# Graph network layer on one core: stages of the main loop set one group of gathers apart, early messages' bias on TensorE and relu on ScalarE

## What is computed

```python
src = node_feature[edge_src]
parts = [jax.nn.relu(node_feature)]
for t in range(n_types):
    msg = jax.nn.relu(src @ W_e[t].T + b_e[t])
    msg = jnp.where((edge_type == t)[:, None], msg, jnp.zeros((), msg.dtype))
    parts.append(jax.ops.segment_sum(msg, edge_dst, num_segments=N))
agg = jnp.concatenate(parts, axis=1)
for t in range(n_types):
    o = agg @ W_n[t].T + b_n[t]
    updated = jnp.where((node_type == t)[:, None], o, updated)
# then: x = layernorm(x + updated + node_feature)
```

## Time and profile before

| What | us |
|---|---|
| median of 3 runs | 922.02 (919.35 to 922.12) |
| span of the profiled execution | 1076.0 |
| PE, DVE, POOL, ACT busy in it | 771.1, 683.5, 671.4, 149.6 |
| mean granted TensorE clock in it | 0.872 |

### The profile page before, as it was taken

How to read it: one execution, slowest core, us unless ns; L and a number is a source line. 1 busy time by engine, 2 the same in 40 slices (tenths; PEclk the granted TensorE clock), 3 DMA queues, 4 the chain that set the end, 5 groups by cost and what they waited for, 6 DMA issues and landing times. The chain is left out here.

```text
span 1076.0 us, 13097 instructions
## 1 busy us (share of the span) xinstructions
PE 771.1 (72%) x4200; PEld 611.8 (57%) x4200; DVE 683.5 (64%) x1539; ACT 149.6 (14%) x397; POOL 671.4 (62%) x718
## 2 busy tenths in 40 slices
PE   5574267777778778777676686888787786778866
PEld 3242156666666566566555565666566565566654
DVE  7997866666555656656566565656656654465645
ACT  2264101101101101100110110011011001111101
POOL 7776655666566666665666665666666666665660
PEclk9697578978898998998999988989888978898898
DMA  7476312422222223223223223223223233132320
GB/s 219 135 256 190 81 50 60 86 72 67 78 80 75 71 77 85 72 70 89 71 70 93 74 67 91 71 67 96 72 67 108 71 105 90 45 93 70 87 57 16
DMA packets 65777, 94.03 MB, mean 87 GB/s; under 512 B 16497, under 2 KB 49233, under 8 KB 65711
## 3 DMA queue, kind: packets, MB, share of 16 engines
q0 software_dynamic: 22432, 45.99, 17.2%
q1 hardware_dynamic: 40577, 43.14, 13.0%
q10 hardware_dynamic: 2702, 4.08, 1.3%
HBM read 80.23 MB, written 12.92 MB: 87 GB/s over the span
## 5 line engine op out<-in xcount | busy, mean ns | idle before, releaser
L619 POOL DMA_INDIRECT tab<-message_table,idx_t x630 | 594.3, 943 | 353.0 <-issue 170.4
L1116 DVE TENSOR_TENSOR work<-key_t,ps 128x378 f32<-128x378 f32 (+1 forms) x180 | 109.5, 610 | 253.1 <-remote 133.0
L1516 PE MATMUL ps<-work,tab 128*128 128x126 f32 x1260 | 197.4, 304 | 35.4 <-DVE acc L1125 20.6
L1516 PEld LDWEIGHTS ps<-work,tab 128*128 128x128 f32 x1260 | 183.3, 219 | 50.3 <-DVE acc L1125 25.5
L1546 PE MATMUL ps<-we_t,order_f 128*128 128x128 f32 x540 | 115.4, 368 | 123.2 <-DVE order_f L1204 84.1
L1546 PEld LDWEIGHTS ps<-we_t,order_f 128*128 128x128 f32 x540 | 93.3, 255 | 135.6 <-DVE order_f L1204 88.8
L1595 PE MATMUL ps<-wn_t,stage 128*128 128x384 f32 x294 | 104.6, 493 | 0.0
L1204 DVE TENSOR_TENSOR order_f<-ps,dst_raw 128x768 f32<-128x768 f32 x45 | 43.1, 957 | 71.7 <-remote 56.7
L615 POOL DMA_INDIRECT xg<-in_x,esrc_t x67 | 71.0, 1060 | 23.9 <-issue 17.7
L1595 PEld LDWEIGHTS ps<-wn_t,stage 128*128 128x128 f32 x294 | 56.3, 193 | 39.7 <-issue 3.1
L747 ACT ACTIVATE dense_f<-ps 128x256 f32<-128x256 f32 x45 | 17.2, 383 | 432.7 <-PE ps L1548 228.8
(11 more groups left out here) (231 smaller groups left out, 952.2 us busy)
## 6 DMA issues: line engine op xcount, KB each, us to landing
tab<-message_table,idx_t POOLq DMA_INDIRECT x630
message_table<-tab SPq DMA_DIRECT2D x24, 384.0 KB
dst_raw<-dense_types SPq DMA_DIRECT2D x45, 192.0 KB
wn_raw<-message_table SPq DMA_DIRECT2D x22, 384.0 KB
src_wide<-dense_lists SPq DMA_DIRECT2D x45, 128.0 KB
xg<-in_x SPq DMA_DIRECT2D x11, 256.0 KB
work<-in_x ACTq DMA_DIRECT2D x10, 256.0 KB
out<-xg SPq DMA_DIRECT2D x10, 256.0 KB
```

Of the source, the lines that this page charges most:

```text
L619: pool.indirect_dma_start(msg[:, slot, :], None, table, bass.IndirectOffsetOnAxis(ap=rows, axis=0)).then_inc(signal, 16)
L1116: dve.tensor_tensor(hot[:, first:first + n, :].rearrange("p c (t w) -> p c t w", w=WIN), keys.broadcast_to((P, n, T, WIN)), iota_win.rearr ...
L1516: ins = pe.matmul(sums_bank(nth), msg[:, column, :], hot[:, column, :], start=(c == 0), stop=(c == n - 1))
```

## The change

Every engine's `iteration` is rewritten, with functions of their own for iterations 0, 1 and the last. In the steady iteration TensorE now does, after g0: `early_make`, `dense_make`; after g1: `dense_turn` of the next iteration; after g2: half of the dense sum, the linear part, `finish_turn`; after g3: the other half, `early_sum`, `early_turn`, `place_selfs`. Between two steps of one item that stand on TensorE there is now at least one group's sum. Groups keep fixed banks (g0 and g2 bank 0, g1 and g3 bank 1); early and dense sums get columns of their own in those banks, and all adds are counted by one semaphore `added`, by a list (`adds_of`). The early messages' bias becomes a bf16 matmul (line 1539 of after), the relu one ScalarE instruction over both chunks, `early_select` and the type masks made for it in setup are gone, and `early_sum` has a matmul for each type and chunk, 42 columns wide. SP loads the next dense lists ahead of the self rows, and the first load of x takes two tiles (`BATCHES`).

```diff
-            link(dve.tensor_copy(etype_i[:, :, :], ekey_t[:, :, :]))
-            link(dve.tensor_scalar(etype_i[:, :, :], etype_i[:, :, :], BITS, None, ALU.logical_shift_right))
             for t in range(T):
-                dve.tensor_scalar(emask[:, :, :, t], etype_i[:, :, :], float(t), None, ALU.is_equal)
...
+            def iteration_one():
...
+                for side in range(SETS):
+                    dense_add(0, side, first_of[2 * side], added_by(1, "p" + str(side)))
+                self_types()
+
+                dve.wait_ge(group_summed, NG + 3)
+                one_hot(2, 2)
+                add_group(1, 2, bases_of[2])
+                dense_mask(1)
+                dense_hot(1)
+
+                dve.wait_ge(group_summed, NG + 4)
+                one_hot(2, 3)
+                dve.wait_ge(e_summed, 1)
+                add_group(1, 3, bases_of[3])
+                early_add(0, bases_of[NG])
+                early_hot(1)
+                self_masks()
+                for side in range(SETS):
+                    dense_add(1, side, bases_of[2 * side], added_by(1, "d" + str(side)))
...
+            def iteration(j, extra=None, last_extra=None):
+                early = j <= NE
+                bases_of = load_bases(j, early)
+
+                dve.wait_ge(group_summed, NG * j + 1)
+                one_hot(j + 1, 0)
+                add_group(j, 0, bases_of[0])
+                dense_onehot(j + 1)
+                finish_acc(j - 2, j - 2, 0, ADDS_BEFORE[j])
                 if j > 2:
...
+                    finish_y(j - 3, j - 3)
+
+                dve.wait_ge(group_summed, NG * j + 2)
+                one_hot(j + 1, 1)
+                add_group(j, 1, bases_of[1])
+                dense_hot(j)
...
+                dve.wait_ge(group_summed, NG * j + 3)
+                one_hot(j + 1, 2)
+                dve.wait_ge(d_summed, SETS * j + 1)
+                add_group(j, 2, bases_of[2])
+                dense_add(j, 0, bases_of[0], added_by(j, "d0"))
+                dense_mask(j + 1)
...
+                dve.wait_ge(group_summed, NG * j + 4)
+                one_hot(j + 1, 3)
+                dve.wait_ge(d_summed, SETS * j + 2)
+                if early:
+                    dve.wait_ge(e_summed, j)
+                add_group(j, 3, bases_of[3])
...
+                finish_h(j - 2, j - 2)
...
+            def early_relu(i):
...
+                act.wait_ge(e_made, i + 1)
+                n = min(2, ET - 2 * i)
+                act.activation(emsg[:, 0:n, :], ps[:, E_MSG_PS[0]:E_MSG_PS[n - 1] + 1, 0:T * D], ACT.Relu
+                               ).then_inc(e_ready, 1)
...
+            def early_make(i):
+                pe.wait_ge(e_copied, i + 1)
+                if i > 0:
+                    pe.wait_ge(e_ready, i)
+                for c in range(min(2, ET - 2 * i)):
+                    pe.matmul(ps[:, E_MSG_PS[c], 0:T * D], xst[:, c, :], we_t[:, :], start=True, stop=False)
+                    ins = pe.matmul(ps[:, E_MSG_PS[c], 0:T * D], pick_parts[:, :], be_parts[:, :], start=False, stop=True)
+                ins.then_inc(e_made, 1)
+
+            def early_sum(i):
+                pe.wait_ge(e_ready, i + 1)
...
+                for t in range(T):
+                    for c in range(n):
+                        ins = pe.matmul(early_sums[:, t * WIN:(t + 1) * WIN], emsg[:, c, t * D:(t + 1) * D],
+                                        ehot[:, c, t * WIN:(t + 1) * WIN], start=(c == 0), stop=(c == n - 1))
+                ins.then_inc(e_summed, 1)
+
+            def sum_group(j, g):
...
+                if g >= 2:
+                    pe.wait_ge(added, added_by(j, "g" + str(g - 2)))
+                elif j > 0:
+                    pe.wait_ge(added, bank_read(j - 1, g))
...
+            def iteration_one():
+                sum_group(1, 0)
+                early_make(0)
+                dense_make(0)
+
+                sum_group(1, 1)
+                for side in range(SETS):
+                    dense_sum(0, side)
+                finish_turn(0, 0, 1, first=True)
+                dense_turn(1)
+
+                sum_group(1, 2)
+                dense_make(1)
+
+                sum_group(1, 3)
+                early_sum(0)
+                early_turn(1)
+                for side in range(SETS):
+                    dense_sum(1, side)
+                spread_types()
+                dense_turn(2)
+
+            def iteration(j, loads, extra=None, last_extra=None):
+                sum_group(j, 0)
+                if j <= NE:
+                    early_make(j - 1)
+                dense_make(j)
...
+                sum_group(j, 1)
+                dense_turn(j + 1)
+
+                sum_group(j, 2)
+                dense_sum(j, 0)
+                finish_linear(j - 2, first=j == 2)
+                finish_turn(j - 1, j - 1, loads)
...
+                sum_group(j, 3)
+                dense_sum(j, 1)
+                if j <= NE:
+                    early_sum(j - 1)
+                if j < NE:
+                    early_turn(j)
+                place_selfs(j - 1, j - 1)
```

More of the change, by code:

```diff
@@ L818, in _ @@
             zero_acc(acc[:, 1, HALF:HALF + 2 * R], 2 * R)
-            iteration(0, True, False)
+            early_copy(0)
             dense_keys()
-            iteration(1, True)
-            for j in range(2, NE):
-                iteration(j, True)
-            for j in range(NE, NI - 1):
-                iteration(j, extra=j - EXTRA_AT if EXTRA_AT <= j < EXTRA_AT + KE else None)
-            iteration(NI - 1, last=True)
+            first_iteration()
+            for j in range(2, NI - 1):
+                iteration(j, extra_of(j), extra_of(j - 1))
+            last_iteration(NI - 1)
             act.wait_ge(ctl_set, 1)
@@ new lines, in iteration_zero @@
+            def iteration_zero():
+                bases_of = load_bases(0, False)
+                for g in range(NG):
+                    dve.wait_ge(group_summed, g + 1)
+                    one_hot(1, g)
+                    add_group(0, g, bases_of[g])
+                early_hot(0)
+                dense_onehot(0)
+            def iteration_one():
+                bases_of = load_bases(1, True)
+                dense_mask(0)
+                dve.wait_ge(group_summed, NG + 1)
+                one_hot(2, 0)
+                add_group(1, 0, bases_of[0])
+                dense_hot(0)
+                dense_onehot(1)
+                dve.wait_ge(group_summed, NG + 2)
+                one_hot(2, 1)
+                add_group(1, 1, bases_of[1])
+                first_of = load_bases(0, False)
+                for side in range(SETS):
[15 more added lines that the diff above has]
+                    dense_add(1, side, bases_of[2 * side], added_by(1, "d" + str(side)))
+                dense_onehot(2)
+                dense_mask(2)
@@ L1366, in _ @@
             dve.wait_ge(acc_zeroed, 1 + 1 + 1 + 1 + 8 + 8)
-            iteration(0)
-            for j in range(1, NI - 1):
-                iteration(j, extra=j - EXTRA_AT if EXTRA_AT <= j < EXTRA_AT + KE else None)
+            iteration_zero()
+            iteration_one()
+            for j in range(2, NI - 1):
+                iteration(j, extra_of(j), extra_of(j - 1))
                 if j == BAD_AT - 1:
@@ L1373, in _ @@
                     decide()
-            iteration(NI - 1, more=False)
+            last_iteration(NI - 1)
             need = dve.value_load(ctl[0:1, 0:1], min_val=0, max_val=1)
@@ L1549, in dense_make, with dense_sum @@
                 ins.then_inc(d_made, 1)
-            def dense_sum(j):
+            def dense_sum(j, side):
                 pe.wait_ge(d_ready, j + 1)
                 pe.wait_ge(d_hot, j + 1)
-                for side in range(2):
-                    ins = pe.matmul(dense_sums(side), dsel[:, side, :], dhot[:, side, :], start=True, stop=True)
-                ins.then_inc(d_summed, 1)
+                pe.matmul(dense_sums(j, side), dsel[:, side, :], dhot[:, side, :], start=True, stop=True
+                          ).then_inc(d_summed, 1)
             def spread_types():
@@ new lines, in iteration_zero @@
+            def iteration_zero():
+                sum_group(0, 0)
+                early_turn(0)
+                for g in range(1, NG):
+                    sum_group(0, g)
+                dense_keys()
+                dense_turn(0)
+            def iteration_one():
[12 more added lines that the diff above has]
+                early_turn(1)
+                for side in range(SETS):
+                    dense_sum(1, side)
+                spread_types()
+                dense_turn(2)
@@ new lines, in last_iteration @@
+            def last_iteration(j):
+                sum_group(j, 0)
+                dense_make(j)
+                finish_turn(ORDER[KE], KE, 2, 1)
+                sum_group(j, 1)
+                finish_linear(j - 2)
+                finish_turn(j - 1, j - 1, len(BATCHES))
+                sum_group(j, 2)
+                for side in range(SETS):
```

(21 more changed lines are left out.)

418 lines of the change are left out of this document (146 added, 272 removed).

## The result

| Kernel | median us | runs | range |
|---|---|---|---|
| before | 921.8 | 18 | 917.4 to 924.4 |
| changed | 928.2 | 18 | 919.9 to 933.2 |

The ratio is 1.0072, with a 95% interval of 1.0051 to 1.0092: 6.4 us slower (4.7 to 8.5). The forecast was 924.0, with 902 to 934 as its range, and 0.30 as the chance that the kernel gets slower by more than 2.8 us.

A forecast was written before the change was run, and what follows sets the result against it. The prediction took the timed loop to be paced by POOL's gathers; all terms counted 0 except setup -0.7 and start +2.7, so 922.0 + 2.0 = 924.0 us, range 902 to 934.

The forecast's parts named there:

- signs named for being right: Median within 3 us, gathers at 943 ns and 0.30, first long stall moving to iteration 2's g3, no TensorE type-mask wait.
- first rival: Main loop: timed runs are paced by POOL's gathers; 924 us, own range 919 to 930, chance 0.55.
- two sums of the long profile: Profiled 1076.0 us less POOL's waits gives 925.6; first gather, 630 gathers and end give 915.8, with two start stalls 928.1.
- second rival: Main loop: TensorE and VectorE pace the timed loop too, so the change is faster, 904 us; chance 0.24.
- VectorE, 36 x 2.9 us less, counted 0: Early messages on VectorE: three instructions go in each of 36 iterations, 2.9 us of 13; 0 in a POOL-paced loop.
- ScalarE, 0: Early messages on ScalarE: one added relu of 797 ns, on an engine busy 2.2 of 20.5 us; 0.
- TensorE, early messages, +1.5 us an iteration: Bias matmuls and twelve narrow sum passes add +0.3 to +2.1 an iteration, under POOL's 17.4; "Covered, barely: 0".
- Stages: New order in the loop: TensorE's 2.70 us wait for the type mask goes; 0 in a loop paced by POOL.
- Moved waits, SyncE, 0: Loop: SP loads dense lists ahead of self rows, both needed a full iteration later; 0.
- Setup, -0.7: Before the loop: casts of the types and three mask instructions go, on the way to VectorE's list work; -0.7 us.
- Start, +2.7: Iteration 1: `dense_make(1)` ahead of g3's sum delays POOL 6.9 us, partly recovered later; +2.7, bounds -0.5 and +6.9.
- third rival: Main loop: added passes and bias matmuls push TensorE over POOL's 17.4 us; slower, 933 or 944 us; chance 0.18.

The follow-up runs named there:

- b_again: The kernel before, unchanged, profiled a second time (the second profile of the kernel before): 920.3 us, span 918.5.
- b_fewer: The kernel before with one gather and one chunk of g3 left out in 44 iterations: 874.9 us, ratio 0.9489 to the kernel before.
- a_fewer: The changed kernel with one gather and one chunk of g3 left out in 44 iterations: 877.1 us, ratio 0.9535 to the kernel before.
- a_select: The changed kernel with early messages made the old way on VectorE, two matmuls in the sum: 924.3 us, ratio 1.0038 to the kernel before.
- b_early: The kernel before with only the early messages' part of the change, order of stages as before: 926.0 us the first time, 922.0 the second.
- a_check: The changed kernel with SyncE's store and load of the row of conditions issued behind iteration 3's other loads: 923.1 us, ratio 1.0037 to the kernel before.
- a_make: The changed kernel with iteration 1's product of dense edges back behind the sum of g3: 924.7 us, ratio 1.0051 to the kernel before.
- a_all: The changed kernel with conditions' transfers later, self loops' types behind iteration 1's mask, iteration 0's adds between listing pieces: 918.4 us, ratio 0.9980 to the kernel before.

## Why the prediction was right, and where it was not

**The time.** 928.2 lies in the forecast's own range of 919 to 930, but the change costs 6.4 us and not 2.0, and that it is slower beyond 2.8 us had 0.13 within the forecast, against 0.40 for the same. Of the signs named for being right, the gathers at 0.94 and 0.30 us and the stall ahead of g3 in iteration 2 came; the median within 3 us did not (4.2 off), and TensorE still waits for the type mask once, 4.55 us.

**The bound** (first rival, paced by POOL): right. The period of 17.48 us is 14 x 1.248; the 1.243 of the sum was 0.005 short. That the 3.3 us between a sum and its release are no part of the kernel's order was right: the second profile has 0.04. That the two sums of the long profile met the median so well (915.8, and 928.1 with two stalls) was partly luck. Its first gather came 6.4 us later and its end took 11.2 us longer than in the second profile, and against that the pace was 3.3 us short in the whole and the stalls of the start were put at 12.3 us where the second profile has 17.0. What the Trainium skill (Perfetto Trace Analysis, "Summary: the profiler window per engine type") says of the estimated end of a matmul would have led to the second rival here; `b_again`, `b_fewer` and `a_fewer` exclude it.

**VectorE, 36 x 2.9 us less, counted 0**: right. 101 us of work went and no gather came sooner.

**ScalarE, 0**: right as far as the steady iterations show it, where no gather waits; its relu takes 0.79 us, as the 0.80 of the earlier trace rows.

**TensorE, early messages, +1.5 us an iteration, "Covered, barely: 0"**: the size was near, the cover is sure only in the loop. The early sum at full clock, of the changed kernel and of the kernel before (second profile):

```profile
182.68 1.43 PE L1548 MATMUL ps<-ehot,emsg 128*128 128x42 f32 x12
```

```profile
172.62 0.71 PE L1506 MATMUL ps<-ehot,esel 128*128 128x126 f32 x4 [0.21 <-DVE esel L1170]
```

The twelve narrow passes take 0.7 us more, and product with bias 1.8 against 1.46, +0.3: 1.0, not 1.5. Less the 0.27 us of the last one, a narrow pass takes 0.105 us, so the forecast's 0.11 for it was right; the two bias matmuls, put at 0.35 us each, overlap and cost 0.3 together. The forecast's "some 17.3 at the granted mean" follows from no row: 15.9 + 1.5 is 17.4 at 0.92, which is POOL's whole pace, and at 0.872 it would be more. What covers it here is the clock: the windows above are at 1.00, with 14.5 to 15.1 us of TensorE in 17.48. What the term left out is the start: in the first iterations TensorE is late and nothing covers added work. `a_select` puts that at 3 to 5 us, `b_early` at 1 to 5, neither well clear of noise.

**Stages**: right. TensorE's wait for the type mask is 4.5 us in all, where the kernel before had 16.4 in its second profile, and it changed nothing in a loop paced by POOL. The page's lines, before (second profile) and after:

```profile
L1546 PE MATMUL ps<-we_t,order_f 128*128 128x128 f32 x540 | 88.8, 305 | 16.9 <-DVE order_f L1204 16.4
```

```profile
L1598 PE MATMUL ps<-we_t,order_f 128*128 128x128 f32 x540 | 83.7, 294 | 4.5 <-DVE order_f L1218 4.5
```

**Moved waits, SyncE, 0**: this step failed, and it is the one whose failure is best shown. I followed the dense lists and the self rows, which did change places at no cost that a profile shows, and not the load of x rows, which the new `BATCHES` moves by one iteration and so behind a store's way to HBM of 7.1 us. `a_check` gives it 4.7 us, by itself as much as the 4.4 us that the forecast of the change was off.

**Setup, -0.7**: not seen. The first gather starts at 101.8 in both profiles of the changed kernel and at 100.7 in that of the one before; other versions with the changed setup have 100.2 to 101.2. If it is there it is below that scatter.

**Start, +2.7**: right in mechanism, and nothing speaks against the size. The stall ahead of g3 in iteration 2 is 6.4 us, as the upper bound of 6.9 had it, some of it is taken back at the start of iteration 3, and `a_make` measures 3.1 net, with the overlap of intervals told above.

**The sum.** The parts that were measured alone (4.7 for SyncE's order, 3.1 for the product's place, 3 to 5 for the early part) add to more than the 6.4. Each is what goes when only it is undone, and the profiles show that with one stall gone a later one grows; noise of some us in each is as large as the excess. They weren't tried two by two, so how the 6.4 us divide among them stays open, as does what the long runs of `b_early` do.

**The third rival**, slower because TensorE becomes the bound of the loop, did not happen: after iteration 5 no gather waits in the changed kernel. The time came out on its side of the forecast for another reason.

## What to carry to other kernels

Where one queue paces the loop, a change to the other engines can only be won or lost in the iterations where that queue still stands, mostly the first: list its waits there one by one, and the whole time is first start, pace times number, waits and tail. Follow every transfer whose issue moves to another iteration, however harmless its own size: in an engine's program it may come to stand behind somebody's store and wait. And profile a kernel twice before its stalls are believed, when the profiled span is far from the timed median. The clock belongs to this too: where TensorE has stood for others at the start, the work behind it takes longer, and so the same program's stalls differ from run to run.

## What was not expected of the hardware

One profiled execution of the same program was 1076.0 us and another 918.5. In the long one's loop the releases by the sums of g1 and g3 came 2.8 to 3.3 us after the matmuls' end, in the short one 0.04 us; no timed run was near the long one. Why that execution was so stays open.

A store of 90 floats to HBM by SyncE took 7.1 us from issue to landing in the changed kernel (190.21 to 197.32), 7.2 in the second profile of the kernel before (183.28 to 190.45) and 6.5 to 8.0 in eleven other profiles. The gathers of the loop, issued by POOL, took 2.4. The Trainium skill (DMA: Bandwidth & Descriptors, "Anatomy of one DMA — SWDGE (gpsimd) path") gives about 2.0 us as the fixed part of a transfer issued by GpSimd, whatever its size. The 2.4 us of the gathers are near it; the store is not issued by GpSimd, so the figure isn't for it, and it takes three times as long.

The spread of a kernel's runs goes with the granted clock: over 75 runs of the kernel before the correlation of time and mean clock is -0.59, with 2.1 us for 0.01 of clock, over 24 of the changed kernel -0.64 and 4.7 us. Over 12 runs of `a_all` it is 1.2 us for 0.01. This fits that more of TensorE's work stands on the path of the changed kernel's start, but is a correlation and doesn't show it.
